# One store counter replaced by four per head parity, with later waits named by group, in the opening stage of a relative-position attention

## Chip, cores and metric

The kernel runs on the 8 cores of one Trainium2 chip, each core on one batch element of 2048 tokens with 1024 features. The metric is the device time of the slowest core, in microseconds (us). Engines: PE is TensorE, ACT ScalarE, DVE VectorE, POOL GpSimd, SP SyncE; a q behind a name is that engine's instruction queue.

## The reference

Two layers are computed, each an attention-like part and a feed-forward part, with a layer norm after each. The change touches only the attention of layer 1, which has 16 heads of 64 features over 2048 tokens, and learned relative positions clipped at 64:

```python
idx = jnp.arange(s)
dist = jnp.clip(idx[None, :] - idx[:, None], -R, R) + R     # R = 64
pe_k = rel_emb_k[dist]
pe_v = rel_emb_v[dist]
qkv = (x @ W_qkv + b_qkv).reshape(b, s, 3, H, hd)
q, k, v = ...                                               # q scaled by 1/sqrt(hd)
score = jnp.einsum('bhqd,bhkd->bhqk', q, k) + jnp.einsum('bhqd,qkd->bhqk', q, pe_k)
attn = jax.nn.softmax(score, axis=-1)
ctx = jnp.einsum('bhqk,bhkd->bhqd', attn, v) + jnp.einsum('bhqk,qkd->bhqd', attn, pe_v)
```

## The kernel before

Everything is written by hand: five lists of instructions, one per engine, each run in order, with semaphores between them. A DMA adds 16 to its semaphore when it has landed. `p.wait(engine, sem, n)` (line 54) makes that engine's queue wait until the semaphore has reached n; if n is left out or is `sem.n`, it is the count of all DMAs that the program has issued on it up to that line. `p.dma` is line 49, and so all DMA issues have that line.

`build_block2` computes the attention, one head `h` after another (`par = h % 2` chooses between two scratch buffers in HBM and their semaphores). A head has an opening stage and four quarters of 512 queries.

The opening stage is a loop over 16 tiles `qt` of 128 queries. PE multiplies the tile's q with the extended table of relative embeddings (L1012) into one of two PSUM banks. ACT copies the 128 x 512 result to one of two SBUF buffers `qrst[0]` and `qrst[1]` (`pp = qt % 2`, L1018) and issues its store of 256 KB to `QRE[par]` (`sc_qre` in the profile; the buffers are called `wm` there). From `qt` 2 on, ACT waits before the copy for `s_qw[par]` at its full present count. After the loop SP waits for PE's last matmul of it and issues four small loads from `sc_mqs`.

At the start of each quarter `qb`, 9 or 10 tiles of up to 128 x 128 are loaded back from `QRE[par]` with a row stride of 511 instead of 512, which shifts each row by one and so lines up the relative positions. Loads with an even index are issued by SP (`s_qr`), those with an odd index by POOL (`s_qrg`). Loads 0 to 3 go to a buffer of their own (`skq`, part of `wj`), loads 4 to 11 to the two `qrst` buffers, from which the stores of the opening stage were sent. Both queues wait first for all stores of the head and for PE's last use of the previous tiles.

In a quarter PE goes over 16 key tiles `kt`: a transposing matmul brings each loaded tile into the scores (L1109; its first one waits for all loads of the quarter), q times k is added (L1114, L1119, L1124), ACT takes the exponential (L1131), and PE multiplies with v (L1136). Then the probabilities near the diagonal are transposed (L1164), copied (L1175), stored to HBM (`sc_e`, by SP and ACT) and loaded back skewed by SP; what follows from these (`b2_tail`, L945 to L982) is put off until `kt` 3 of the next quarter or head. SP's list for a quarter is: tile loads, stores of `sc_e`, wait, loads of `sc_e`.

Of the kernel before, what the change touches and what calls it, by code (L numbers as in the profile page):

```python
# [535 lines left out]
def build_block2(p, es, B):  # L536
# [16 lines left out]
    s_wv = [p.sem("s_wv0"), p.sem("s_wv1")]  # L553
    s_wo = p.sem("s_wo")
    s_qw = [p.sem("s_qw0"), p.sem("s_qw1")]
    s_qr = [p.sem("s_qr0"), p.sem("s_qr1")]
    s_qrg = [p.sem("s_qrg0"), p.sem("s_qrg1")]
    s_bt = p.sem("s_bt")
# [70 lines left out]
    qrst = [wm[5][:, 0:D].bitcast(F32)[:, 0:512], wm[0][:, 0:D].bitcast(F32)[:, 0:512]]  # L629
# [358 lines left out]
    for h in range(NH):  # L988
        par = h % 2
# [15 lines left out]
        qw_done = [0, 0]  # L1005
        for qt in range(NTT):
            pp = qt % 2
            bank = pb[:, 512 + pp * 512:1024 + pp * 512]
            if qr_ev[pp]:
                p.wait("tensor", s_se, qr_ev[pp])  # L1010
            p.op("tensor", lambda q, o=bank, t=qt:
                 q.matmul(o, QELt[0:128, 128 * t:128 * (t + 1)],  # L1012
                          wj[0][0:128, 2048:2560], start=True, stop=True), s_tr)
            t_tok = p.sems["s_tr"].n
            p.wait("scalar", s_tr, t_tok)
            if qw_done[pp]:
                p.wait("scalar", s_qw[par], s_qw[par].n)
            p.op("scalar", lambda q, o=qrst[pp], i_=bank: q.activation(out=o, in_=i_, func=AF.Copy), s_se)  # L1018
            qr_ev[pp] = p.sems["s_se"].n
            p.wait("scalar", s_se, qr_ev[pp])  # L1020
            p.dma("scalar", bass.AP(QRE[par].tensor, 128 * qt * 512, [[512, 128], [1, 512]]),
                  qrst[pp], s_qw[par])
            qw_done[pp] = s_qw[par].n
        qw_tok = s_qw[par].n
        p.wait("tensor", s_se, p.sems["s_se"].n)
        p.wait("sync", s_ve, cp_tok)
        p.wait("sync", s_ld2, s_ld2.n)
# [10 lines left out]
        for qb in range(NQB):  # L1038
# [15 lines left out]
                        tlist.append((kt, c0, cw))  # L1054
                        c0 += cw
            assert len(tlist) <= 12
            p.wait("sync", s_qw[par], qw_tok)
            p.wait("sync", s_tr, last_skq_use)
            p.wait("gpsimd", s_qw[par], qw_tok)
            p.wait("gpsimd", s_tr, last_skq_use)  # L1060
            for idx, (kt, c0, cw) in enumerate(tlist):
                p.dma("sync" if idx % 2 == 0 else "gpsimd", tstg[idx][0:cw, 0:128],
                      bass.AP(QRE[par].tensor, c0 * 511 + 128 * kt + 256, [[511, cw], [1, 128]]),
                      s_qr[par] if idx % 2 == 0 else s_qrg[par])
# [6 lines left out]
            for kt in range(NTT):  # L1071
# [7 lines left out]
                pp = kt % 2  # L1079
# [17 lines left out]
                for oi, op_ in enumerate(ops):  # L1097
                    st = (oi == 0)
                    sp = (oi == nops - 1)
                    if op_[0] == "T":  # L1100
                        _, c0, cw = op_
# [4 lines left out]
                        idx, _cw = tchunks[(kt, c0)]  # L1106
# [3 lines left out]
                    elif op_[0] == "R":  # L1110
                        _, a0, a1 = op_
# [3 lines left out]
                    elif op_[0] == "B":  # L1115
                        _, a0, a1 = op_
# [3 lines left out]
                    else:  # L1120
                        _, a0, a1 = op_
# [61 lines left out]
            for qtl in range(4):  # L1183
                qt = qb * 4 + qtl
# [6 lines left out]
            for qtl in range(4):  # L1191
                qt = qb * 4 + qtl
# [1015 lines left out]
def build_program(n_blocks=1):  # L2208
# [71 lines left out]
    with es:  # L2280
# [61 lines left out]
        if n_blocks >= 3:  # L2342
            build_block2(p, es, B)
# [49 lines left out]
```

How the kernel before makes its waits and increments, by code:

```python
    def dma(self, eng, out, in_, sem):  # L47
        sem.n += 16
        self.on(eng, lambda q, o=out, i=in_, s=sem: q.dma_start(out=o, in_=i).then_inc(s.h, 16))
# [1 line left out]
    def wait(self, eng, sem, val=None):  # L51
        v = sem.n if val is None else val
        if v > 0:
            self.on(eng, lambda q, s=sem, vv=v: q.wait_ge(s.h, vv))
# [1 line left out]
    def op(self, eng, fn, sem=None, k=1):  # L56
        if sem is not None:
            sem.n += k
            self.on(eng, lambda q, f=fn, s=sem, kk=k: f(q).then_inc(s.h, kk))
            return sem.n
        self.on(eng, lambda q, f=fn: f(q))
        return None
```

## Time and profile before

| | us |
|---|---|
| median of 2 runs | 10401.8 |
| the runs | 10370.4 and 10433.2 |
| the profiled execution | 10427.8 |
| its span, slowest core (7) | 10426.2 |
| its spans, all cores | 10364.1 to 10426.2 |
| mean granted TensorE clock, all cores | 0.632 to 0.636 |

The rows further down are from the slowest core of the profiled execution. Times in them are microseconds from the start of the span, where a number is marked ns or is the mean of one instruction, nanoseconds. Busy time leaves out the issuing of DMAs by ACT and SP and the waits. The 16 heads of the attention begin between 1704 and 5808 us; head 0 begins at 1704, head 9 at 4153, heads 10 and 11 at 4430 and 4706.

### The profile page before, as it was taken

The page shows a single profiled execution, that of the slowest core. Times are in us where ns is not written, and L with a number is a line of the kernel's source. Part 1 is how long each engine was busy: PE and PEld are TensorE (multiplying, and loading weights), DVE is VectorE, ACT ScalarE, POOL GpSimd, SP SyncE. Part 2 cuts the span into 40 slices and gives each one's busy share as a digit, 9 for nine tenths or more (in the row PEclk, how much of TensorE's full clock was granted, in tenths as well). Part 3 has the DMA queues.
Part 4 walks back from the last instruction along what each step waited for, and adds up shares of the span by engine and source line. Part 5 has one row for each costly group of instructions (what it writes and reads, how often), then busy time and mean ns, then how long its engine had stood idle before and what let it go on. Part 6 is the DMA issues. An engine that isn't in the chain of part 4 may idle for free.

```text
span 10426.2 us, 59672 instructions; the slowest of 8 cores (10364.1 to 10426.2 us)
## 1 busy us (share of the span) xinstructions
PE 5278.3 (51%) x19111; PEld 2010.1 (19%) x19111; DVE 2730.8 (26%) x3977; ACT 1670.9 (16%) x3009; POOL 840.3 (8%) x813
## 2 busy tenths in 40 slices
PE   4353463554555555544454563334449743444894
PEld 2111121111111111111111121011114311111341
DVE  5756302000000000000000012543351144334214
ACT  2100011222222222222222200011101001110100
POOL 0000000000000000000000000211111112111010
PEclk8675795555555555555555576555569865555896
DMA  3000230111111111111111112000004210000331
GB/s 57 9 4 0 48 43 25 38 34 38 38 37 38 34 33 35 30 37 38 38 34 37 38 49 51 6 1 0 0 7 39 32 13 0 1 1 5 29 32 65
DMA packets 458420, 285.22 MB, mean 27 GB/s; under 512 B 307482, under 2 KB 403995, under 8 KB 454027
## 3 DMA queue, kind: packets, MB, share of 16 engines
q0 software_dynamic: 222240, 81.89, 7.0%
q1 hardware_dynamic: 180588, 120.34, 4.5%
q10 hardware_dynamic: 55296, 79.19, 2.1%
q8 instruction: 168, 2.75, 0.1%
q14 instruction: 128, 1.05, 0.1%
HBM read 227.39 MB, written 118.96 MB: 33 GB/s over the span
## 4 chain that ended last, share of the span: by engine, by line
PE 42%; DVE 17%; DMA 17%; ACT 11%; issue 6%; SPq 3%; DVEq 1%; POOL 1%; ACTq 1%; POOLq 0%; PEldq 0%; PEld 0%
DMA sc_amax<-amaxc 7%; PE pm L1136 5%; ACT xb L1131 5%; DMA sc_qre<-wm 5%; PE pm L1919 3%; PE pb L1940 3%; SPq L49 3%; DVE wm L971 2%; PE pm L1114 2%; PE pm L1429 2%; PE pb L1149 2%; PE pm L1985 2%; PE pb L1985 2%; PE pb L1733 2%; ACT wm L1018 1%
## 5 line engine op out<-in xcount | busy, mean ns | idle before, releaser
L971 DVE RECIPROCAL wm<-pm 1x512 f32<-1x512 f32 x64 | 214.5, 3352 | 3637.0 <-PE pm L967 3637.0
L1131 ACT ACTIVATE xb<-pm 128x512 bf16<-128x512 f32 x1024 | 611.4, 597 | 1998.2 <-PE pm L1124 1211.4
L1136 PE MATMUL pm<-xb,U 128*65 128x512 bf16 x576 | 342.6, 595 | 604.9 <-ACT xb L1131 604.9
L49 POOL DMA_DIRECT2D wj<-sc_qre x128 | 70.5, 553 | 4298.8 <-PE pm L1119 2354.9
L1012 PE MATMUL pb<-wj 128*128 128x512 bf16 x256 | 142.1, 566 | 517.9 <-ACT wm L1018 482.2
L1698 DVE TENSOR_REDUCE amaxc<-pm 128x1 f32<-128x640 f32 (+4 forms) x256 | 181.7, 740 | 791.2 <-PE pm L1694 789.6
L1744 ACT ACTIVATE xb<-pb 128x512 bf16<-128x512 f32 x448 | 243.3, 595 | 577.0 <-PE pb L1733 577.0
L1114 PE MATMUL pm<-qer,wj 128*128 128x512 bf16 (+4 forms) x576 | 308.2, 535 | 0.0
L1124 PE MATMUL pm<-wj 128*128 128x512 bf16 (+4 forms) x576 | 290.9, 505 | 0.0
L220 PE MATMUL pm<-xb,wj 128*128 128x512 bf16 x512 | 138.8, 439 | 283.9 <-ACT U L231 261.5
L1721 PE MATMUL pb<-wm,zbuf 1*65 1x512 bf16 x64 | 38.6, 603 | 467.2 <-DMA wj<-sc_amax 467.2
L1136 PE MATMUL pm<-xb 128*65 128x512 bf16 x256 | 155.6, 608 | 215.2 <-ACT xb L1131 215.2
L1136 PEld LDWEIGHTS pm<-xb,U 128*65 128x65 bf16 x576 | 74.1, 129 | 939.4 <-issue 939.4
L1617 DVE RECIPROCAL wm<-pb 1x512 f32<-1x512 f32 x64 | 214.5, 3352 | 150.1 <-PE pb L1613 149.6
L1018 ACT ACTIVATE wm<-pb 128x512 f32<-128x512 f32 x256 | 152.9, 597 | 555.3 <-DMA sc_qre<-wm 527.0
L1919 PE MATMUL pm<-xb,wm 128*128 128x512 bf16 (+1 forms) x704 | 188.5, 392 | 99.4 <-DVE xin L1867 99.4
L1429 PE MATMUL pm<-xb,wm 128*128 128x512 bf16 x384 | 111.0, 416 | 223.3 <-DVE xin L1401 172.3
L49 POOL DMA_DIRECT2D wm<-l1f_w x152 | 128.1, 850 | 1028.2 <-PE pm L1919 519.3
L1136 PE MATMUL pm<-xb,vex 128*65 128x512 bf16 x192 | 116.6, 607 | 161.5 <-ACT xb L1131 161.5
L1109 PE MATMUL pm<-identf,wj 128*128 128x128 f32 (+1 forms) x256 | 94.2, 398 | 202.0 <-DMA wm<-sc_qre 202.0
L1149 PE MATMUL pb<-xb,onesbc 128*1 128x512 bf16 (+4 forms) x576 | 190.8, 502 | 0.0
L1175 ACT ACTIVATE xb<-pb 128x384 bf16<-128x384 bf16 (+1 forms) x256 | 101.4, 482 | 531.1 <-PE pb L1164 531.1
(435 smaller groups left out, 9464.3 us busy)
## 6 DMA issues: line engine op xcount, KB each, us to landing
sc_qre<-wm ACTq DMA_DIRECT2D x256, 256.0 KB, 2.1
xb<-sc_e SPq DMA_DIRECT2D x256, 128.0 KB, 2.4
wm<-l1f_w POOLq DMA_DIRECT2D x116, 256.0 KB, 4.2
sc_xspill<-xr SPq DMA_DIRECT2D x16, 1024.0 KB, 13.8
wm<-W_qkv POOLq DMA_DIRECT2D x48, 256.0 KB, 4.3
sc_e<-xb ACTq DMA_DIRECT2D x112, 96.0 KB, 2.1
sc_e<-xb SPq DMA_DIRECT2D x112, 96.0 KB, 1.9
xin<-x SPq DMA_DIRECT2D x16, 512.0 KB, 3.7
```

The source lines that it names most:

```text
L49: self.on(eng, lambda q, o=out, i=in_, s=sem: q.dma_start(out=o, in_=i).then_inc(s.h, 16))
L971: p.op("vector", lambda q, c2=ctxp: q.reciprocal(out=srow[0:1, 0:512], in_=c2[64:65, 0:512]))
L1018: p.op("scalar", lambda q, o=qrst[pp], i_=bank: q.activation(out=o, in_=i_, func=AF.Copy), s_se)
L1114: q.matmul(o, l, r, start=s1, stop=s2), s_tr)
L1124: q.matmul(o, l, r, start=s1, stop=s2), s_tr)
L1131: q.activation(out=o, in_=i_, func=AF.Exp), s_se)
L1136: q.matmul(o, l, r, start=st, stop=False), None)
L1149: q.matmul(o, onesbc[:], r, start=False, stop=False), None)
L1429: q.matmul(o, l, r, start=st, stop=sp),
L1919: q.matmul(o, l, r, start=st, stop=sp),
L1940: q.matmul(o, l, r, start=st, stop=sp),
L1985: q.matmul(o, l, r, start=st, stop=sp),
```

## The change

`s_qw[par]` isn't used any more for the stores of the opening stage. Each parity gets four semaphores `s_qw4[par][g]`, one for each group of four stores, `g = qt // 4`. Before tile `qt` (from 2 on) ACT waits for group `(qt - 2) // 4` at its present count. At the start of quarter `qb`, SP and POOL wait for group `qb` alone, issue loads 0 to 3, and then wait for all four groups before load 4.

```diff
--- before.py
+++ after.py
@@ -553,6 +553,7 @@
     s_wv = [p.sem("s_wv0"), p.sem("s_wv1")]
     s_wo = p.sem("s_wo")
     s_qw = [p.sem("s_qw0"), p.sem("s_qw1")]
+    s_qw4 = [[p.sem(f"s_qw4_{par}_{g}") for g in range(4)] for par in range(2)]
     s_qr = [p.sem("s_qr0"), p.sem("s_qr1")]
     s_qrg = [p.sem("s_qrg0"), p.sem("s_qrg1")]
     s_bt = p.sem("s_bt")
@@ -1013,15 +1014,15 @@
                           wj[0][0:128, 2048:2560], start=True, stop=True), s_tr)
             t_tok = p.sems["s_tr"].n
             p.wait("scalar", s_tr, t_tok)
-            if qw_done[pp]:
-                p.wait("scalar", s_qw[par], s_qw[par].n)
+            if qt >= 2:
+                g2 = (qt - 2) // 4
+                p.wait("scalar", s_qw4[par][g2], s_qw4[par][g2].n)
             p.op("scalar", lambda q, o=qrst[pp], i_=bank: q.activation(out=o, in_=i_, func=AF.Copy), s_se)
             qr_ev[pp] = p.sems["s_se"].n
             p.wait("scalar", s_se, qr_ev[pp])
             p.dma("scalar", bass.AP(QRE[par].tensor, 128 * qt * 512, [[512, 128], [1, 512]]),
-                  qrst[pp], s_qw[par])
-            qw_done[pp] = s_qw[par].n
-        qw_tok = s_qw[par].n
+                  qrst[pp], s_qw4[par][qt // 4])
+        qw_grp = [s_qw4[par][g].n for g in range(4)]
         p.wait("tensor", s_se, p.sems["s_se"].n)
         p.wait("sync", s_ve, cp_tok)
         p.wait("sync", s_ld2, s_ld2.n)
@@ -1054,11 +1055,17 @@
                         tlist.append((kt, c0, cw))
                         c0 += cw
             assert len(tlist) <= 12
-            p.wait("sync", s_qw[par], qw_tok)
+            p.wait("sync", s_qw4[par][qb], qw_grp[qb])
             p.wait("sync", s_tr, last_skq_use)
-            p.wait("gpsimd", s_qw[par], qw_tok)
+            p.wait("gpsimd", s_qw4[par][qb], qw_grp[qb])
             p.wait("gpsimd", s_tr, last_skq_use)
+            allw = False
             for idx, (kt, c0, cw) in enumerate(tlist):
+                if idx == 4 and not allw:
+                    for g in range(4):
+                        p.wait("sync", s_qw4[par][g], qw_grp[g])
+                        p.wait("gpsimd", s_qw4[par][g], qw_grp[g])
+                    allw = True
                 p.dma("sync" if idx % 2 == 0 else "gpsimd", tstg[idx][0:cw, 0:128],
                       bass.AP(QRE[par].tensor, c0 * 511 + 128 * kt + 256, [[511, cw], [1, 128]]),
                       s_qr[par] if idx % 2 == 0 else s_qrg[par])
```

## Rows read from the trace of the kernel before

**Rows 1.** The page of the slowest core: part 4 by line, part 5 for L1018.

```profile
DMA sc_amax<-amaxc 7%; PE pm L1136 5%; ACT xb L1131 5%; DMA sc_qre<-wm 5%; PE pm L1919 3%; PE pb L1940 3%; SPq L49 3%; DVE wm L971 2%; PE pm L1114 2%; PE pm L1429 2%; PE pb L1149 2%; PE pm L1985 2%; PE pb L1985 2%; PE pb L1733 2%; ACT wm L1018 1%
...
L1018 ACT ACTIVATE wm<-pb 128x512 f32<-128x512 f32 x256 | 152.9, 597 | 555.3 <-DMA sc_qre<-wm 527.0
```

**Rows 2.** The view of line L1109: idle us before it, times.

```profile
its engine sat idle before it (us, times) until:
...
  DMA wm<-sc_qre: 202.0, 16
```

**Rows 3.** Busy time by stretch; the last three columns are clock, DMA share, GB/s.

```profile
4166.00:4180.00 14.00, 2.93 (x5) 0.52 (x5) 0.00 (x0) 2.99 (x6) 0.00 (x0) 0.50 0.25 94
...
4156.00:4204.00 48.00, 7.62 (x13) 1.34 (x13) 0.00 (x0) 8.36 (x14) 2.16 (x4) 0.50 0.34 107
```

**Rows 4.** Chain that ended last, head 9's opening stage: start us, us, what.

```profile
4168.20 0.02 ACTq L54
4168.22 0.04 issue
4168.26 0.61 ACT wm L1018
...
4168.94 2.02 DMA sc_qre<-wm
...
4171.72 2.04 DMA sc_qre<-wm
...
4191.47 2.08 DMA sc_qre<-wm
...
4194.31 2.09 DMA sc_qre<-wm
...
4197.16 2.04 DMA sc_qre<-wm
...
4201.40 3.39 DMA wm<-sc_qre
```

**Rows 5.** The same chain, head 0: its first stores and the last tile load.

```profile
1706.01 0.34 ACTq L49
...
1707.13 2.15 DMA sc_qre<-wm
...
1710.04 2.15 DMA sc_qre<-wm
...
1750.93 2.86 DMA wm<-sc_qre
```

**Rows 6.** Timeline: `sc_e` loads (head 9); issues of stores 1, 2 (heads 10, 11).

```profile
4155.83 2.00 SPq L49 DMA_DIRECT2D xb<-sc_e  x4
...
4432.08 0.33 ACTq L49 DMA_DIRECT2D sc_qre<-wm  x1
...
4435.40 0.33 ACTq L49 DMA_DIRECT2D sc_qre<-wm  x1
...
4707.82 0.34 ACTq L49 DMA_DIRECT2D sc_qre<-wm  x1
...
4712.92 0.33 ACTq L49 DMA_DIRECT2D sc_qre<-wm  x1
```

**Rows 7.** Timeline, end of head 9's opening stage.

```profile
4199.31 0.82 SPq L49 DMA_DIRECT2D wj<-sc_qre  x2
4199.78 1.10 POOL L49 DMA_DIRECT2D wj<-sc_qre  x2 [114.19 <-DMA sc_qre<-wm]
...
4204.92 0.74 PE L1109 MATMUL pm<-identf,wj 128*128 128x128 f32 x2 [12.80 <-DMA wm<-sc_qre]
```

**Rows 8.** Timeline, SP, the last two `sc_mqs` loads of head 9.

```profile
4192.88 0.72 SPq L49 DMA_DIRECT2D qer<-sc_mqs  x2
```

**Rows 9.** DMA issues by line: count, KB each, median us to landing.

```profile
wm<-sc_qre POOLq DMA_DIRECT2D x112, 64.0 KB, 2.2
```

**Rows 10.** Timeline, quarter 1 of head 9: SP's last tile loads, PE's first transpose.

```profile
4264.50 1.53 SPq L49 DMA_DIRECT2D wm<-sc_qre  x3
...
4278.67 0.36 PE L1109 MATMUL pm<-identf,wj 64*128 64x64 f32 x1
```

## The prediction

> **What bounds the kernel now.** I began with the page's chain that ended last and its costliest groups [rows 1]. The longest single line holds 7% of the chain, so no engine is the bound: the kernel is a chain of latencies, and 5% of it is landing of the stores `sc_qre<-wm` that the change touches. ScalarE's copy L1018 runs 256 times (16 heads by 16 tiles) and sat idle 555.3 us before it, 527.0 of that for those stores. PE's first transposes L1109 waited 202.0 us for the tile loads `wm<-sc_qre`, 16 times, once per head, 12.6 us each [rows 2]. So the stage that opens each head of block 2 is where the change acts, and little else runs there: from 4156 to 4204 PE is busy 7.62 us and ScalarE 8.36 us of 48 [rows 3].
>
> Then the chain in order of time gives one step of the store loop [rows 4]: 0.61 us copy (4168.26), 0.07 us to the issue, 2.02 us to landing (4168.94), 0.08 us to the next copy. The issues lie 2.78 us apart at 4171.72 and 2.85 at 4197.16; I take 2.83 for a step.
>
> **The waits that the change relaxes.** The old code waits before tile 2 and every later tile for the count of *all* stores issued so far: 14 waits per head. The new wait names group g2 = (qt-2)//4 at its present count. Written out: tile 2 waits for stores 0 and 1; tile 3 for 0 to 2; tile 4 for 0 to 3; tile 5 still for 0 to 3, so not for store 4. Tile 6 waits for 4 and 5, and so on. Only tiles 5, 9 and 13 no longer wait for the store right before them; the other 11 waits of the 14 still do. That is 3 relaxed steps a head, 48 in all.
>
> What a relaxed step is worth can be read in the old trace, because tile 1 never waited for store 0. In head 0, with no other traffic beside it, the issues are at 1706.01, 1707.13 and 1710.04 [rows 5]: 1.12 us and then 2.91 us. The second store landed after 2.15 us [rows 5], against 2.02 to 2.09 in the plain steps [rows 4]. The new tile 5 carries one wait that tile 1 hadn't; a satisfied wait is 0.02 us and 0.04 us of issue [rows 4], 0.06 us. The pair costs 1.12 + 0.06 + 2.91 = 4.09 us where two plain steps cost 5.66: 1.57 us less. I take 1.55. 48 x 1.55 = 74 us. PE's matmul for a relaxed tile waits only for the copy two tiles back, so it is ready. Upper bound: the second store lands in 2.04 us, 1.66 us a pair, 80 us. Lower bound: the same pair in the 15 later heads, where the previous head's `sc_e` stores and loads run beside it, had second steps between 3.32 us (head 10) and 5.10 us (head 11) [rows 6], 4.2 in the middle. With 4.2 a pair saves 5.66 - 1.18 - 4.2 = 0.28 us, 13 us in all. I take nearly the upper one. That `sc_e` traffic is issued from 4155.83 to 4157.83 [rows 6] and is over before tile 5, some 12 us into the stage. And the engines have room: in plain steps the DMA share is 0.25 [rows 3], so 0.7 us of moving in each 2.8 us, and two transfers need 1.4 us of a 4.09 us pair.
>
> The trace puts a 256 KB store at 2.02 to 2.09 us [rows 4]. The Trainium skill (DMA: Bandwidth & Descriptors, Anatomy of one DMA) fits a DMA of GpSimd's queue as about 2.0 us, mostly the wait for the write receipt, plus bytes over 436 GB/s; for 256 KB that is an estimated 2.6 us, more than this case's trace has on ScalarE's queue, and the trace decides. By that figure a plain step would be 3.4 us and a pair would save an estimated 2.25 us, 108 us instead of 74.
>
> **The loads that move.** For the first quarter (qb 0) nine tiles are loaded, five from SP and four from POOL. Before, all nine wait for the last store: issued at 4197.16 and landed 2.04 us later [rows 4]; SP issues from 4199.31 (0.82 us for two, so about 0.45 apart with the gap), POOL from 4199.78 (1.10 us for two), and PE starts at 4204.92 [rows 7]. In head 9 the chain goes through POOL's last load, 3.39 us to landing [rows 4]; in head 0 through SP's fifth, issued at 1750.93, 2.86 us to landing [rows 5]. After, two loads of each queue go ahead: POOL's as soon as group 0 has landed, SP's once the four `sc_mqs` loads are out, which in the old order is at 4192.88 + 0.72 [rows 8], 5.6 us before the last landing. That takes 2 x 0.45 = 0.9 us off SP's row and 1.10 us off POOL's. The smaller counts, since both must end: 0.9. With five loads instead of nine in the burst each should also land sooner. Bounds for that: nothing, and 3.39 - 2.2 = 1.2 us (2.2 is POOL's median for this load [rows 9]). I take 0.3, so 1.2 us a head, 16 x 1.2 = 19 us, from 14 to 34.
>
> The early loads run beside stores that everything waits for. Each head gets two bursts of two tiles, 96 to 128 KB. Lower bound of the cost: nothing, as the four `sc_mqs` loads (tiny, 4 KB each) leave the stores beside them at 2.08 and 2.09 us [rows 4, 8]. Upper bound: what the whole `sc_e` traffic does, four loads of 128 KB and four stores of 64 or 96 KB, namely 4.2 - 2.9 = 1.3 us [rows 5, 6]; 2 x 16 x 1.3 = 42 us. A burst is about an eighth of those bytes, so I take 0.2 us, 32 x 0.2 = 6 us.
>
> **Costed at nothing, and by what cover.** Each quarter gets four more waits on SP and on POOL ahead of the fifth tile, 0.06 us each when satisfied [rows 4]: 0.24 us. On quarters 1 to 3 every store has long landed. Behind these waits are the remaining tile loads and then the `sc_e` stores. SP ends its tile issues for quarter 1 at 4264.50 + 1.53 = 4266.03, and PE reads the first tile at 4278.67, 12.6 us later [rows 10]; less some 2.2 us of landing, 10 us stay. POOL doesn't stand behind the `sc_e` work and issues earlier. SP's next work is the `sc_e` stores of the quarter just begun, most of a quarter away. If the cover were gone, 48 x 0.24 = 12 us. PE's granted clock is 0.50, its lower level of 1.2 GHz, in the whole store stage [rows 3], with no matmul on the path, so a shorter stage changes nothing there. What is late next: PE behind the last five tile loads, as before; the pending part of the last quarter isn't needed until tile kt 3.
>
> **Sum.** 74 + 19 - 6 = 87 us. The profiled execution took 10427.8 us and would take 10341; the median of the runs is 26 us lower, 10401.8, and gives 10315 us, 0.8% less. This is inside the 2% that I take as about what a measurement of this kernel can tell from no change.
>
> **Rivals.**
> *The early loads hold up the stores.* For: the `sc_e` traffic visibly does that to store 1 [rows 6]. Against: far fewer bytes, and `sc_mqs` shows none [rows 4, 8]. Time: 10401.8 - 74 - 19 + 42 = 10350. The Trainium skill (DMA: Bandwidth & Descriptors, Queues, rings and completion order) gives a mechanism for it: a completion increment lands only after every earlier write of that DMA engine, across its queues, so a store's completion could wait for a tile load's data. By that rule the time would be near this rival's; the trace can be read so for `sc_e`, and not for `sc_mqs`.
> *The pairs don't overlap.* Outside head 0 the second store of a pair was always late. If that lateness belongs to the pair and not to `sc_e`, 13 us remain of 74: 10401.8 - 13 - 19 + 6 = 10376. Head 0 speaks against it.
> *Slower than before.* Same place, larger size: two stores in flight each time hinder each other. It decides from a second step of 5.66 - 1.18 = 4.48 us on, plus 13/48 = 0.27 for what the tail gives, so 4.75 us, which only heads near 5.10 reach [rows 6]. At 5.10: 48 x 0.62 = 30 us lost, less 13: 10419. To be 2% slower it would need 9 us a step, which no row has.
> *The wait is really two deep.* If all 14 steps ran two buffers deep, a step would be half of 0.61 + 0.15 + 2.08, 1.42 us: 14 x 16 x 1.41 = 316 us, so 10073, 3.2% faster. The counts written out above exclude it: 11 of 14 waits still name the store just issued.
>
> **How the numbers follow.** Forecast 0.74, hindered stores 0.14, no overlap 0.06, slower 0.03, two deep 0.03. The likeliest case alone spans 80 + 34 = 114 us gained (10288) to a pair at 1.4 us and bursts at 0.4: 67 + 15 - 13 = 69 us (10333). The two runs of before lie 31 us either side of their median, and a median of the new kernel can be as far off: 10257 to 10364. The hindered case at 10350 lies in it; taking in part of the no-overlap case I give 10260 to 10368. Faster by over 2%: 0.03, the two-deep case. Slower by over 2%: 0.02, for what I don't see. Within 2%: 0.95.
>
> **What the new profile would show.** The issues of `sc_qre<-wm` 1.17 us apart before tiles 5, 9 and 13, then about 2.9 us, all others still 2.8 (two deep would show 1.4 throughout; no overlap, a step over 4 after each pair). The idle time of L1018 down from 555 by about 75 us. First to last store issue in a quiet head down from about 41 us to 36.5. POOL's two `wj<-sc_qre` some 30 us before the last landing, and steps over 3 us next to them if they hinder. Last landing to PE's first L1109, 5.7 us in head 9 [rows 4, 7], down to about 4.5. If PE's wait at L1109 in quarter 1 names a DMA, the cover that I relied on is gone. The forecast is wrong if the spacing is as said but the span isn't shorter by 60 us or more: then something later took it back.

## The result, and the profile after

| us | before | changed |
|---|---|---|
| median of the runs | 10385.7 (10 runs) | 10284.2 (11 runs) |
| lowest and highest | 10362.2 and 10581.8 | 10119.1 and 10448.0 |
| span of the slowest core, profiled execution | 10426.2 | 10276.4 |

The ratio of changed to before is 0.9835, with a 95% interval of 0.9775 to 0.9895: 1.65% less, or 171 us, where 87 were forecast. The ratio compares means and, like every spread given below, leaves out executions over 1.5% above the fastest of their kernel or with one half of the chip over 1% longer at a lower clock; the single one at 10119.1 us puts eight of the changed kernel's eleven over that bound, and only three remain (10261.9, 10266.8 and 10119.1). The medians of all runs lie 101.5 us apart.

The page of the slowest core, core 3, shows what became of the two groups that the prediction started from: the chain by line, L1018 (now L1020) of [rows 1], and, in the view of the transposes' line, L1109 (now L1116) of [rows 2].

```profile
DMA sc_amax<-amaxc 7%; PE pm L1143 5%; ACT xb L1138 5%; DMA sc_qre<-wm 4%; PE pm L1926 3%; PE pb L1947 3%; SPq L49 3%; DVE wm L972 2%; PE pm L1121 2%; PE pm L1436 2%; PE pb L1156 2%; PE pb L1740 2%; PE pm L1992 2%; PE pb L1992 2%; ACT wm L1020 2%
...
L1020 ACT ACTIVATE wm<-pb 128x512 f32<-128x512 f32 x256 | 153.0, 598 | 485.5 <-DMA sc_qre<-wm 430.0
```

```profile
its engine sat idle before it (us, times) until:
...
  DMA wm<-sc_qre: 177.5, 16
```

ScalarE's idle time fell from 555.3 to 485.5 us, 70 us, and PE's wait for the tile loads from 202.0 to 177.5. The 16 opening stages, from first to last store issue, took 42.4 us on average on the slowest core before and 38.1 after; from the last store issue to PE's first transpose 7.6 and 5.6. That is 6.3 us a head, about 100 us.

The timeline of head 0 on core 3 (ScalarE's issues of stores 4, 5 and 6, then the end of the stage on SP, POOL and PE) can be laid beside [rows 5, 7, 8].

```profile
1717.48 0.33 ACTq L49 DMA_DIRECT2D sc_qre<-wm  x1
...
1718.64 0.33 ACTq L49 DMA_DIRECT2D sc_qre<-wm  x1
...
1722.21 0.33 ACTq L49 DMA_DIRECT2D sc_qre<-wm  x1
...
1727.79 0.33 ACTq L49 DMA_DIRECT2D sc_qre<-wm  x1
...
1728.95 0.33 ACTq L49 DMA_DIRECT2D sc_qre<-wm  x1
...
1731.79 0.33 ACTq L49 DMA_DIRECT2D sc_qre<-wm  x1
```

```profile
1740.73 0.81 SPq L49 DMA_DIRECT2D wj<-sc_qre  x2
1746.71 1.35 SPq L49 DMA_DIRECT2D wm<-sc_qre  x3
1747.17 1.07 POOL L49 DMA_DIRECT2D wm<-sc_qre  x2 [28.79 <-DMA sc_qre<-wm]
...
1750.07 0.74 PE L1116 MATMUL pm<-identf,wj 128*128 128x128 f32 x2 [10.89 <-DMA wm<-sc_qre]
```

Tile 5 follows tile 4 after 1.16 us, and tile 9 follows tile 8 after 1.16, as worked out in the prediction. The pair at tile 9 takes 1.16 + 2.84 = 4.00 us, the one at tile 5 1.16 + 3.57 = 4.73, since POOL's first two loads run beside it. The chain of the same stretch (start us, us, what) puts numbers on the two bursts of early loads.

```profile
1718.64 2.82 DMA sc_qre<-wm
...
1738.53 2.07 DMA sc_qre<-wm
1741.35 2.50 DMA sc_qre<-wm
...
1744.61 2.03 DMA sc_qre<-wm
...
1747.70 2.23 DMA wm<-sc_qre
```

Stores next to a burst landed after 2.82 and 2.50 us, the others after 2.03 to 2.08.

So the opening stage did what the forecast said. What doesn't fit the 171 us is outside it. The spans of the eight cores of this execution:

```profile
core 0: 10265.6 us, clock 0.639
core 1: 10268.0 us, clock 0.638
core 2: 10273.3 us, clock 0.637
core 3: 10276.4 us, clock 0.636
core 4: 10055.5 us, clock 0.643
core 5: 10069.4 us, clock 0.639
core 6: 10087.4 us, clock 0.641
core 7: 10106.3 us, clock 0.641
```

The cores go in pairs (0 and 1, 2 and 3, and so on), and pairs differ by 200 us. The difference is in block 3, the local attention of the last layer, where each of 64 windows sends its row maxima through HBM: four stores of 4-byte elements `sc_amax<-amaxc` from SP, one load `wj<-sc_amax` from POOL, and then PE's opening matmul L1728 (L1721 before). Groups by line and DMA issues (count, KB, median us to landing): first core 3, then core 4, both of the changed kernel.

```profile
L1728 PE MATMUL pb<-wm,zbuf 1*65 1x512 bf16 x64 | 38.6, 603 | 473.2 <-DMA wj<-sc_amax 473.2
...
sc_amax<-amaxc SPq DMA_DIRECT2D x272, 0.5 KB, 9.2
wj<-sc_amax POOLq DMA_DIRECT2D x64, 1.0 KB, 1.8
```

```profile
L1728 PE MATMUL pb<-wm,zbuf 1*65 1x512 bf16 x64 | 38.6, 603 | 296.1 <-DMA wj<-sc_amax 296.1
...
sc_amax<-amaxc SPq DMA_DIRECT2D x272, 0.5 KB, 6.6
wj<-sc_amax POOLq DMA_DIRECT2D x64, 1.0 KB, 2.2
```

PE waits 473 us on core 3 and 296 on core 4, 177 of the 221 us between them. I call a pair high or low by this wait. In the profiled execution of before all four pairs were high (467 to 488 us on the eight cores), so its trace held no low pair to compare with.

High pairs have a second mark. In each high pair of both traces one core has the slow stores and a fast load (9.0 to 9.2 and 1.8 to 1.9 us), and its partner has faster stores and the slow load (6.4 and 4.2 to 4.4 us); no core of a low pair has either (stores 5.9 to 6.7, load 1.9 to 2.2). So the two cores of a high pair pay for the same exchange in different places.

### The profile page after: what moved, and what is told of

Read it like the earlier page. It is cut to its first block, busy times and chain, and to the rows that moved or that the text cites. A ratio compares the mean times of both kernels' runs of the same rounds, so it can differ in the third digit from the quotient of the medians.

```text
span 10276.4 us, 60184 instructions; the slowest of 8 cores (10055.5 to 10276.4 us)
## 1 busy us (share of the span) xinstructions
PE 5232.6 (51%) x19111; PEld 1999.8 (19%) x19111; DVE 2731.3 (27%) x3977; ACT 1671.4 (16%) x3009; POOL 840.1 (8%) x813
## 4 chain that ended last, share of the span: by engine, by line
PE 43%; DVE 18%; DMA 16%; ACT 12%; issue 6%; SPq 3%; DVEq 1%; ACTq 1%; POOL 1%; POOLq 0%; PEldq 0%; PEld 0%
DMA sc_amax<-amaxc 7%; PE pm L1143 5%; ACT xb L1138 5%; DMA sc_qre<-wm 4%; PE pm L1926 3%; PE pb L1947 3%; SPq L49 3%; DVE wm L972 2%; PE pm L1121 2%; PE pm L1436 2%; PE pb L1156 2%; PE pb L1740 2%; PE pm L1992 2%; PE pb L1992 2%; ACT wm L1020 2%
## 5 line engine op out<-in xcount | busy, mean ns | idle before, releaser
L1728 PE MATMUL pb<-wm,zbuf 1*65 1x512 bf16 x64 | 38.6, 603 | 473.2 <-DMA wj<-sc_amax 473.2
L1020 ACT ACTIVATE wm<-pb 128x512 f32<-128x512 f32 x256 | 153.0, 598 | 485.5 <-DMA sc_qre<-wm 430.0
L1182 ACT ACTIVATE xb<-pb 128x384 bf16<-128x384 bf16 (+1 forms) x256 | 101.5, 484 | 526.6 <-PE pb L1171 526.6
L1116 PE MATMUL pm<-identf,wj 128*128 128x128 f32 (+1 forms) x256 | 94.1, 398 | 177.5 <-DMA wm<-sc_qre 177.5
```

## The experiments

Two theories stood after the comparison, with the letters that the expectation of e1 gives them. A: the change itself moves pairs into the low mode. B: it works in the opening stage alone, for about 90 us, and the rest of the 171 is which pairs happened to be low. (The expectation of e5 uses the letters A and B anew, for what makes the pairs differ.) "Lowest pair" below is the least span, over all executions of a kernel on a chip, of the slower core of a pair.

**e1, the kernel before again, and e2, the changed kernel again.**

> The kernel before, unchanged, for the spans of all eight cores in several executions. In the one profiled execution of before all eight cores lie at 10364 to 10426 us; in the changed kernel each pair of cores (0 and 1, 2 and 3, 4 and 5, 6 and 7) lies either at 10055 to 10130 or at 10250 to 10300 us, and the difference sits in block 3, in the exchange through sc_amax (25.0 against 22.2 us per window, 62 windows). Theory A (the change frees block 3): before has no or almost no pair that is about 200 us below the others. Theory B (chance that the maximum over cores hides): before has pairs near 10180 us as often as the changed kernel has pairs near 10080, about half of them. Both expect a median of 10385 us.

> The changed kernel again, on the same chip as the kernel before: how often a pair of cores is in the lower mode, and what the time is like for like. Theory of the opening stage (mode left aside): executions with at least one pair in the upper mode take 100 us less than before, 10285 us; an execution with all four pairs in the lower mode about 10120 us. Store stage per head, first to last store, 38 us against 42.4; head period 266 against 274 us on the slowest core.

Measured: e1 0.9971 of before (0.9939 to 1.0002). The same kernel against itself came out 0.3% apart, here and again in e10, so a ratio is no better than that. Levels don't carry over from the first measurement: on this chip before has a median of 10515 us and not the expected 10385, and in e1 to e11 PE's wait is 365 to 429 us in low pairs and 524 to 578 in high ones (e5, e6, e8 and e9 apart). Only kernels on one chip are compared from here on.

The 12 executions of e1 and 17 more of before on that chip have pairs from 10257 to 10601 us. So low pairs occur in the kernel before too, and the maximum over cores hides them: not one execution had all four within 60 us of the lowest. Theory A in its strict form, that before has none, falls.

e2 took 0.989 (0.9848 to 0.9931), medians 10396 against 10515. Lowest pair: 10171 changed, 10257 before, 86 us. Within 60 us of the lowest lay 26 of 116 pairs before and 10 of 24 changed, which left a weaker form of theory A open: that low pairs are more frequent with the change. A least value falls with the number of draws, and before has more of them, so the 86 us is if anything too small.

**e3, the relaxed waits alone, and e4, the early loads alone.** e3 against the changed kernel waits for all groups before load 0:

```diff
-            p.wait("sync", s_qw4[par][qb], qw_grp[qb])
-            p.wait("gpsimd", s_qw4[par][qb], qw_grp[qb])
-            allw = False
+            for g in range(4):
+                p.wait("sync", s_qw4[par][g], qw_grp[g])
+                p.wait("gpsimd", s_qw4[par][g], qw_grp[g])
+            allw = True
```

e4 against the changed kernel waits for the store right before, always:

```diff
-                g2 = (qt - 2) // 4
+                g2 = (qt - 1) // 4
```

> Only the relaxed waits of the store loop; SP and POOL wait for all four groups before load 0, as before. By the sum of the prediction: three pairs per head at 1.16 and 2.85 us instead of two steps of 2.83, 1.65 us each, 48 of them, 79 us; without the early tile loads the second step of the first pair should be 2.85 instead of 3.2 and the last step 2.83 instead of 3.3 us, so first to last store 37.2 us. Time in the upper mode 10385 - 79 = 10306 us. If the early loads carry most of the gain it would be above 10340.

> Only the early loads: ScalarE waits for the store right before each tile, as before; loads 0 to 3 of a quarter wait for their group alone. By the prediction: 19 us gained in the tail and 6 to 13 lost where the loads run beside stores, so 10375 us in the upper mode, within 0.2% of before. If the moved loads are worth more than was said, below 10355. Whether pairs fall into the lower mode here tells whether any shift in the opening stage does that, or only the shorter store loop.

Measured: e3 0.9888 (0.9849 to 0.9927), median 10395, lowest pair 10165; e4 0.990 (0.985 to 0.9949), median 10452, lowest pair 10257. By the lowest pairs the waits alone bring 92 us, the loads alone nothing; by its ratio e4 brings 1%, but that hangs on the modes. In e4's profiled execution all pairs were low in block 3, and the slowest pair owes its 70 to 105 us over the others to the part after the last window, 999 us against some 911, where core 7's granted clock was 0.82 (9700 to 9900 us) and core 0's 1.00. So pairs can differ at the end of the kernel too (e2's cores 0 and 1 have 972 us there).

The stages give a measure that the modes don't touch. The averages over the 16 heads and all eight cores of each profiled execution:

| us per head | e1 before | e4 loads | e3 waits | e2 both |
|---|---|---|---|---|
| first to last store issue | 41.56 | 42.17 | 36.41 | 37.35 |
| last store issue to first transpose | 7.24 | 5.69 | 7.19 | 5.69 |
| sum | 48.81 | 47.87 | 43.60 | 43.05 |
| head 0's first store to block 3's first window, us in all | 5075.8 | 5057.0 | 4984.5 | 4975.2 |

The slowest core alone would mislead here: on one and the same chip and kernel the stages differ by up to 0.9 us a head between cores, which is as much as the loads bring. The loads take 1.5 us off the tail and put 0.6 (e4) to 0.9 us (e2 beside e3) on the stores. So they bring 0.9 us a head alone and 0.55 beside the waits, 15 and 9 us in all; by the last row it is 19 and 9, and 91 for the waits alone. In e3, without a burst beside it, store 6 follows store 5 of head 0 after the plain 2.79 us (timeline of core 5: issues of stores 5, 6 and 7), where the changed kernel took 3.57:

```profile
1755.52 0.33 ACTq L49 DMA_DIRECT2D sc_qre<-wm  x1
...
1758.31 0.33 ACTq L49 DMA_DIRECT2D sc_qre<-wm  x1
...
1761.11 0.33 ACTq L49 DMA_DIRECT2D sc_qre<-wm  x1
```

**e5 and e6, block 3's exchange without HBM,** on before and on the changed kernel (left out: VectorE's wait at the head of a window, which goes from `smb` to `smg`). Both the stores to HBM and the load from it go:

```diff
-            p.wait("sync", s_ve, neg_tok)
-            p.wait("sync", smg[b], smg[b].n)
-            for qt in range(4):
-                p.dma("sync", bass.AP(scb.tensor, scoff[b] + qt * 128, [[1, 128], [1, 1]]),
-                      mcs[b][:, qt:qt + 1], smb[b])
-            p.wait("gpsimd", smb[b], smb[b].n)
+            p.wait("gpsimd", s_ve, neg_tok)
...
-            p.dma("gpsimd", qe_ap(b, 64, 65, 0, 512),
-                  bass.AP(scb.tensor, scoff[b], [[512, 1], [1, 512]]), smg[b])
+            for qt in range(4):
+                p.dma("gpsimd", qe_ap(b, 64, 65, qt * 128, (qt + 1) * 128),
+                      mcs[b][:, qt:qt + 1], smg[b])
```

> The kernel before with one edit in block 3 only: the window maxima no longer go out to HBM by four stores of 4-byte elements from SP and back by one load from POOL; POOL moves the four columns from SBUF to SBUF itself. Theory A (the pairs of cores differ because their exchanges through sc_amax collide in the HBM that the two share): the spread between the four pairs of an execution falls from 100 to 300 us to under 60, and PE's wait at the opening matmul of a window, 4.6 to 8.8 us now, falls under 2 us; that is 64 x 4 to 7 us, so the lowest pairs go from 10260 to about 9950. Theory B (the modes come from elsewhere, the clock or the large loads): the spread stays at 100 to 300 us whatever the exchange does.

> The same edit in block 3 on the changed kernel. With the modes gone the two kernels can be compared cleanly. Theory of the opening stage: this one is 90 us below e5_sbuf_before, the difference of the lowest pairs so far (10260 against 10171), within 20 us. If the change had also worked on block 3, as the ratio of the first measurement (171 us) suggests, the difference here would be clearly smaller than the 120 us between the medians of before and changed on this chip, or clearly larger than 90 if it worked elsewhere.

Measured: e5 0.9588 (0.9542 to 0.9634), median 10067.8; e6 0.9511 (0.9452 to 0.9569), median 9982.1. The spread between the pairs of one execution fell to a median of 55 us in e5 and 51 in e6, from 138 in before on the same chip. PE's wait at the window's opening, in the groups by line of e5:

```profile
L1717 PE MATMUL pb<-wm,zbuf 1*65 1x512 bf16 x64 | 38.6, 603 | 104.5 <-DMA wj<-amaxc 60.1 <-DVE xb L1631 44.4
```

104.5 us in place of 467 in the trace of before, 1.6 us a window. With the modes gone the medians of the two kernels differ by 10067.8 - 9982.1 = 85.7 us. Six executions each don't fix that closely: e5's lie between 10031 and 10132 us, e6's between 9949 and 10133; without the last one it is 90 us, and the lowest pairs (10004.7, where 9950 was expected, and 9903.1) are 102 us apart.

The traces do better, since each stretch can be taken alone, averaged over eight cores. From the first window of block 3 to the last it is 2311.2 us in e5 and 2312.5 in e6: the change does nothing to block 3. From head 0's first store to that first window it is 5106.7 and 4991.8 us, 115 less. The other three pairs of traces of before and changed give 113 (first measurement), 101 (e1, e2) and 109 (e10, e11). The opening stages hold 6.2, 6.1, 5.8 and 5.7 us a head of it, 91 to 98 us; the few us beyond were not traced, and the rest of a head differs by as much between traces of before itself (222.1 to 223.6 us). So the change is worth some 90 to 115 us, about 1%.

The edit shows another thing: the two cores of a pair, which had ended within 5 us of each other (median), now end 16 to 18 us apart. The exchange had held them together.

**e7, two stores deep throughout, and e8, the same with e6's edit.** e7 against the changed kernel (the waits of SP and POOL left out):

```diff
+    s_qwb = [[p.sem(f"s_qwb_{par}_{k}") for k in range(2)] for par in range(2)]
...
             if qt >= 2:
-                g2 = (qt - 2) // 4
-                p.wait("scalar", s_qw4[par][g2], s_qw4[par][g2].n)
+                p.wait("scalar", s_qwb[par][pp], s_qwb[par][pp].n)
...
-                  qrst[pp], s_qw4[par][qt // 4])
+                  qrst[pp], s_qwb[par][pp])
```

(SP and POOL wait for the two counts after tile 3 before the first loads, and for the final counts before load 4.)

> The changed kernel, but one semaphore per staging buffer instead of one per group of four stores: each tile waits for the store two back and for nothing else, all 14 waits relaxed instead of 3. By the row of the plain steps a step is half of 0.61 + 0.15 + 2.08, 1.42 us, as the rival of the prediction said: first to last store 21 us against 38, 16 x 17 = 270 us less than the changed kernel, lowest pairs 9900, median near 10130. If several stores in a row in flight hinder each other, steps of 1.8 us or more and under 200 us.

> Both edits together, as the candidate that should beat both kernels: 270 us less than e6_sbuf_after, that is 360 us less than e5_sbuf_before, if the two edits lie in different stages and don't touch each other.

Measured: e7 0.9703 (0.9632 to 0.9775; three of its six executions enter it), median 10290, lowest pair 9931, 351 us under the lowest of before on that chip. Its median is 160 us over the expected 10130, with six of the eight cores of its profiled execution in high pairs (PE's wait 524 to 578 us). e8 0.9298 (0.924 to 0.9355), median 9753.5, which is 229 us below e6 and 314 below e5: 7% faster than before. The 270 us that were expected came out as 229, and as 215 in the stretch from head 0's first store to block 3. Steps in the timeline of e7's slowest core, head 3:

```profile
2475.81 0.33 ACTq L49 DMA_DIRECT2D sc_qre<-wm  x1
...
2477.04 0.33 ACTq L49 DMA_DIRECT2D sc_qre<-wm  x1
...
2478.60 0.33 ACTq L49 DMA_DIRECT2D sc_qre<-wm  x1
...
2479.82 0.33 ACTq L49 DMA_DIRECT2D sc_qre<-wm  x1
...
2481.43 0.33 ACTq L49 DMA_DIRECT2D sc_qre<-wm  x1
```

1.23 and 1.56 us in turn, 1.40 on average: the expected 1.42. What is missing lies at tiles 2 to 5, beside the `sc_e` traffic and POOL's early loads, where single steps of 2 to 2.8 us remain; the stage takes 23.3 us instead of 21, and the tail 6.4 instead of 5.7.

**e9, the 4-byte stores of block 3 doubled,** the second copies to a part of `sc_amax` that nobody reads.

```diff
             for qt in range(4):
+                p.dma("sync", bass.AP(scb.tensor, scoff[b] + 512 + qt * 128, [[1, 128], [1, 1]]),
+                      mcs[b][:, qt:qt + 1], smb[b])
```

> The kernel before with each of the four 4-byte-element stores of a window in block 3 issued twice, the second copy to an unused part of sc_amax: a dose of what is suspected. The output is unchanged. If the pairs of cores differ because their 4-byte stores collide, twice as many of them makes PE's wait at the opening of a window longer by more than the issue of four more DMAs (four times about 0.45 us of SP, so 64 x 1.8 = 115 us), 64 x 6 us or more, and the spread between the pairs grows from 140 to 215 us to about 300. If the stores are not the cause, the time rises by about 115 us and the spread stays.

Measured: 1.0297 (1.0254 to 1.0339), median 10826; the spread between pairs rose from 192 us (before, same chip) to 371. Lowest pair 10378, 116 above the lowest of before in that chip's 23 executions beside it, as the four more issues alone should cost (115); PE's wait in low pairs rose likewise, from 390 to 411 us in e10 to 507 to 513. The groups by line and the DMA issues of core 2, a low pair, and of core 6, a high one:

```profile
L1723 PE MATMUL pb<-wm,zbuf 1*65 1x512 bf16 x64 | 38.6, 603 | 513.1 <-DMA wj<-sc_amax 513.1
...
wj<-sc_amax POOLq DMA_DIRECT2D x64, 1.0 KB, 2.0
```

```profile
L1723 PE MATMUL pb<-wm,zbuf 1*65 1x512 bf16 x64 | 38.6, 604 | 845.7 <-DMA wj<-sc_amax 845.7
...
wj<-sc_amax POOLq DMA_DIRECT2D x64, 1.0 KB, 4.3
```

333 us between low and high, where e11 on the same chip has 145 (average waits of 554 and 408 us), and the first measurement 177. Twice the stores, about twice the gap, with the load unchanged: what a high pair pays hangs on the 4-byte stores to HBM. The second mark is there too: stores of 12.3 and 12.6 us with loads of 1.9 on one core of each high pair, 7.8 and 7.6 with 4.3 on the other. Why a pair is high in one execution and low in the next isn't shown by this.

**e10 and e11, before and changed once more,** to settle what was left of theory A.

> The kernel before once more, for the spans of its pairs of cores beside those of the changed kernel. If the change leaves block 3 alone, the lowest pairs are about 90 us above those of e11_after_third, and the share of pairs within 60 us of the lowest is the same in both kernels. On the chip of e1 and e2 it was about 25% before and 46% after, of 116 and 24 pairs.

> The changed kernel once more. If it leaves block 3 alone: lowest pairs 86 to 90 us below the kernel before, median of the slowest cores 90 to 120 us below, and as many pairs near the lowest as before. If the change does loosen the coupling of the pairs, the share of low pairs is again about twice that of before and the medians differ by more than 120 us.

Measured: e10 0.9968 (0.9935 to 1.0001), e11 0.9922 (0.9884 to 0.9959), medians 10499 and 10430, 69 us apart where 90 to 120 were expected. Lowest pair 10257.3 and 10170.8, again 86 us apart. Within 60 us of the lowest: 29 of 140 pairs before, 10 of 48 changed, 21% both. The 42% of e2 didn't come back; over both chips it is 55 of 256 against 20 of 72. Theory A has no support left: a small shift can't be excluded by these counts, but the equal window stretches of e5 and e6 speak against any work of the change in block 3.

## Why the prediction was right and wrong

**Which waits are relaxed:** right. 1.16 us before tiles 5, 9 and 13 in each of the 16 heads, and about 2.8 us elsewhere, apart from tile 1 and the steps beside other traffic. The two-deep rival is excluded, and e7 shows what it would have been worth.

**What a relaxed step is worth:** too small. With no burst beside it the second store lands in the plain time, so a pair costs 1.16 + 2.79 = 3.95 us (e3) and not 4.09. The stage and its tail shrink by 5.2 us a head, 83 us (e1 to e3), the whole stretch up to block 3 by 91, and the lowest pairs by 92; the sum had 74.

**The no-overlap and slower rivals:** wrong, as head 0 had said. The lateness of store 1 in the other heads belongs to the `sc_e` traffic, since the pairs at tiles 9 and 13 don't have it.

**The loads that move:** each part was too small, and the net a little too large. The tail gave 1.5 us a head and not 1.2. But the bursts cost 0.6 to 0.9 us a head and not 0.4: the scaling by bytes to an eighth failed, since in head 0 two loads of 64 KB slow a store by 0.4 to 0.8 us. Beside the relaxed waits the net is 9 us where 13 were put. The Trainium skill's ordering rule, weighed in the rival (DMA: Bandwidth & Descriptors, Queues, rings and completion order), agrees in direction with stores of 2.50 and 2.82 us beside a burst, but the rival's full price of 42 us wasn't paid; it was 10 to 15.

**Waits costed at nothing:** right. In the changed kernel PE waited for a DMA at L1116 16 times, once per head, so the quarters 1 to 3 kept their cover.

**The sum:** 87 us forecast; 92 by the stages of e1 and e2, 101 to 115 by the stretch up to block 3, 86 to 102 by the lowest pairs. The mechanism was right and the size a little low. That it came so close is in part luck, since two errors inside it partly cancelled: 83 or more for 74, and 9 for 13.

**The step that failed** is the one behind the sum, the range. The ratio of 0.9835 on 10401.8 us is 10230 us, 30 us under its lower end of 10260. "The two runs of before lie 31 us either side of their median, and a median of the new kernel can be as far off" took everything outside the opening stage as fixed to within 31 us. It isn't: each pair of cores draws block 3 at a cost that varies by some 150 to 180 us, and the time is the maximum of four draws. In the first measurement of before no run was under 10362 us, where the high pairs of its trace ended at 10365 to 10426, so at least one pair was high in each, and the same held for ten of the changed kernel's eleven. The eleventh, 10119 us, had all four low, is 143 and 148 us below the two others that entered the ratio, keeps the rest out of it, and so makes the 101 us of the medians into 171 of the ratio. Without it, the mean of the two others, 10264, against before's 10387 is 1.2%. So the 1.65% is not what the change is worth; about 1% is.

Could the trace of before have told? Only in part. The line with the largest share of its chain was `sc_amax<-amaxc`, 7% [rows 1]; the prediction mentions it only as "the longest single line" and then leaves it alone. And the DMA issues of two cores, both high, differ in a way that one core's page doesn't show: core 7, then core 4.

```profile
sc_amax<-amaxc SPq DMA_DIRECT2D x272, 0.5 KB, 9.1
wj<-sc_amax POOLq DMA_DIRECT2D x64, 1.0 KB, 1.9
```

```profile
sc_amax<-amaxc SPq DMA_DIRECT2D x272, 0.5 KB, 6.4
wj<-sc_amax POOLq DMA_DIRECT2D x64, 1.0 KB, 4.3
```

The same small transfer takes 1.9 us on one core and 4.3 on another, for the same program, and core 7's own partner, core 6, has 6.4 and 4.4 like core 4. It is so in all four pairs. That the cores of a pair are coupled, and that a time outside the change could move, was there to be seen, and was reason for a wider range.

## What to carry to other kernels

Read a wait by its count: a group semaphore at its present count still names the store just issued, and only the tiles where the group lags gain; one semaphore per buffer relaxes all of them (14 waits instead of 3, some 220 us more here). Before a forecast, look at all cores and not only the slowest: where a kernel's exchange through HBM is on the path, the time is a maximum of draws, and a change of 1% has to be measured with that exchange taken out, between the lowest draws, or stretch by stretch in the traces, averaged over all cores. A single very short execution can carry a ratio. Loads issued early beside a store that everything waits for can cost half of what they save.

## What the runs showed of the hardware

With an exchange through HBM by stores of 4-byte elements, the two cores of a pair move together. With it they end about 5 us apart (median) while pairs differ by 134 to 230 us in the median execution of a kernel (e1 to e4, e7, e10, e11); twice the stores make it 371; without them it is 51 to 58, and the two cores drift 13 to 18 us apart. The Trainium skill (DMA: Bandwidth & Descriptors, Specifications) has two facts that fit, that two NeuronCores share an HBM stack and that transfers below 512 B are done as read-modify-write. That the collision takes place between the two cores of one pair is argued from this, from their equal spans and from the mark of the high pairs, slow stores on one core and the slow load on the other (in every high pair of the traces but one of e7, cores 4 and 5, which have 8.6 and 2.9 us, 7.1 and 3.6); no experiment idled one core, so it isn't shown. What puts a pair into the one mode or the other wasn't found, nor what lengthens single pairs elsewhere: the end of the kernel in e4, and in e10 the windows of cores 6 and 7, 2677 to 2681 us against 2572 to 2596 on the other cores, with the wait of a low pair (390 to 400 us).

Two 256 KB stores from one queue 1.16 us apart land as fast as one alone (2.07 us, against 2.03), and five in a row still keep steps of 1.40 us. A load burst of two 64 KB tiles beside such a store delays it by 0.4 to 0.8 us.
